# Token mixing: gated products in groups of four tiles instead of two, with the rest of a batch's work one place later

## The reference, cut to what matters

```python
q = x @ Wq + bq
k = x @ Wk + bk
v = x @ Wv + bv
scores = jnp.einsum('btd,bsd->bts', q, k)
retained = jnp.einsum('bts,bsd->btd', d_gamma_batched * scores, v)
y = retained @ Wo + bo
out = jnp.where(y >= 0, y, prelu_a * y)
```

## Time and profile before

| | us |
|---|---|
| median of 3 runs | 3925.51 (3924.63 to 3928.59) |
| the profiled execution's own time | 3921.38 |
| its span, first to last instruction | 3919.6 |
| mixing: starts of the first gating and of the last step (L589) | 40.74 and 396.84 |
| from one batch's `yT` to the next, undisturbed (226.80 to 247.25) | 20.45 |
| mean granted TensorE clock | 0.986 |

### The profile page before, as it was taken

One profiled execution on the slowest core, in us unless ns is written; L12 is line 12 of the kernel. 1 busy time (PEld: TensorE's weight loads), 2 busy tenths in 40 slices (PEclk: granted clock), 3 DMA queues, 4 the chain that ended last, 5 costly groups with the idle time before them and its releaser, 6 DMA issues. The chain is left out here.

```text
span 3919.6 us, 159989 instructions
## 1 busy us (share of the span) xinstructions
PE 3750.3 (96%) x61932; PEld 2749.2 (70%) x61932; DVE 3139.5 (80%) x21227; ACT 2391.9 (61%) x11882; POOL 85.4 (2%) x129
## 2 busy tenths in 40 slices
PE   7899999999999999999999899999999999999998
PEld 3333888888888888888888666666666666666664
DVE  6999899999999999999998677766777667776675
ACT  3232898888889889888887344444444443444443
POOL 6100000000000000000000000000000000000000
PEclk8999999999999999999999999999999999999999
DMA  3111000000000000000000000000000000000000
GB/s 91 22 25 23 3 3 3 3 3 3 3 3 3 3 3 3 3 3 3 3 3 4 4 8 8 8 6 6 8 8 8 6 7 7 8 8 6 6 8 7
DMA packets 49571, 34.01 MB, mean 9 GB/s; under 512 B 37661, under 2 KB 46877, under 8 KB 48806
## 3 DMA queue, kind: packets, MB, share of 16 engines
q1 hardware_dynamic: 48806, 23.77, 2.3%
HBM read 15.37 MB, written 8.39 MB: 6 GB/s over the span
## 5 line engine op out<-in xcount | busy, mean ns | idle before, releaser
L740 PE MATMUL bank<-xs,ident 128*128 128x128 f16 x15583 | 1415.1, 223 | 0.0
L740 PEld LDWEIGHTS bank<-xs,ident 128*128 128x128 f16 x15583 | 1010.2, 102 | 252.2 <-issue 229.8
L760 ACT ACTIVATE ifg_cell_dec<-bank 128x48 f32<-128x48 f32 x1024 | 215.2, 210 | 641.3 <-PE bank L752 641.3
L752 PE MATMUL bank<-enc_lo,u_hi 128*128 128x16 f16 x8192 | 530.1, 173 | 0.3 <-DVE enc_lo L812 0.3
L749 PE MATMUL bank<-enc_hi,u_lo 128*128 128x16 f16 x8192 | 527.8, 173 | 0.0
L775 DVE SCALAR_TENSOR_TENSOR terms_dec<-ifg_cell_dec 128x32 f32<-128x32 f32 x1024 | 197.1, 193 | 398.3 <-ACT ifg_cell_dec L760 387.2
L749 PE MATMUL bank<-enc_hi,u_hi 128*128 128x16 f16 x8192 | 501.6, 170 | 0.0
L749 PEld LDWEIGHTS bank<-enc_hi,u_lo 128*128 128x128 f16 x8192 | 338.4, 96 | 205.6 <-DVE enc_hi L806 171.2
L767 ACT ACTIVATE bank<-twice_cell_dec 128x16 f32<-128x16 f32 x1024 | 191.7, 187 | 402.4 <-DVE twice_cell_dec L781 402.4
L752 PEld LDWEIGHTS bank<-enc_lo,u_hi 128*128 128x128 f16 x8192 | 339.3, 96 | 67.9 <-DVE enc_lo L812 0.4
L749 PE MATMUL bank<-ring_hi,u_lo 128*128 128x16 f16 x4096 | 260.7, 172 | 102.3 <-DVE ring_hi L806 96.0
(11 more groups left out here) (268 smaller groups left out, 7900.8 us busy)
## 6 DMA issues: line engine op xcount, KB each, us to landing
g_rows<-tok_d_gamma_batched_dram SPq DMA_DIRECT2D x8, 512.0 KB, 6.5
x_rows<-in_x_dram SPq DMA_DIRECT2D x16, 256.0 KB, 3.0
kept_h<-tok_ln_h SPq DMA_DIRECT2D x32, 128.0 KB, 2.1
res<-kept_h SPq DMA_DIRECT2D x32, 128.0 KB
out_dram<-sums SPq DMA_DIRECT2D x32, 128.0 KB
raw_wd<-in_L_attn_Wd_dram SPq DMA_DIRECT2D x2, 256.0 KB
raw_experts<-in_L_ffn_W_dram SPq DMA_DIRECT2D x2, 256.0 KB
raw_u<-in_L_attn_Uf_dram SPq DMA_DIRECT2D x1, 256.0 KB
```

The lines of the kernel that those rows point to most:

```text
L740: nc.tensor.matmul(spare, m.ident16[:], m.xs[:, 0, :, :].rearrange("p b t -> p (b t)"), start=False, stop=True, skip_group_check=True)
L752: last = nc.tensor.matmul(z[k], m.u_hi[c.d][:, g, :], h_lo, start=False, stop=True, skip_group_check=True)
L760: nc.scalar.activation(c.ifg_cell[:, 0:3, :], ifg, ACT.Tanh, scale=1.0 / Z_SCALE).then_inc(c.s_t_ifg, 1)
```

## The change

Products are issued in groups of four tiles: at places 3, 7, 11 and 15 of a batch, the group of tiles t - 7 to t - 4. Before, a pair of tiles t - 3 and t - 2 was issued at each odd place. At place 3 the group is thus tiles 12 to 15 of the batch before. `G_RING` goes from 6 to 8. Every piece of `post` on PE, ACT and DVE is moved from place t to t + 1, because the last products of a batch now come at place 3. `Z_RING` stays 3, `prep` stays where it was, and no arithmetic is added or taken out.

```diff
     Z_RING = 3
-    G_RING = 6
+    G_RING = 8
+    GROUP = 4
...
-                def product_pair(n):
-                    pe.wait_ge(s_g, n + 2)
-                    product(*divmod(n, NT))
-                    product(*divmod(n + 1, NT))
+                def product_group(n):
+                    pe.wait_ge(s_g, n + GROUP)
+                    for k in range(n, n + GROUP):
+                        product(*divmod(k, NT))
 
                 def products(b, t):
 
-                    n = NT * b + t - 3
-                    if t % 2 and n >= 0:
-                        product_pair(n)
+                    n = NT * b + t + 1 - 2 * GROUP
+                    if n >= 0 and n % GROUP == 0:
+                        product_group(n)
 
                 def last_products():
-                    product_pair(NT * B - 2)
+                    product_group(NT * B - GROUP)
...
                 def post(b, t):
                     k = b % 2
-                    if t == 3:
+                    if t == 4:
                         pe.wait_ge(s_yT, b + 1)
...
-                    if t == 2:
+                    if t == 3:
                         act.wait_ge(s_av, NT * (b + 1))
                         S.activation(yT[:], m.bank[3 + k][:], ACT.Identity, bias=m.bo_col[:, 0:1]).then_inc(s_yT, 1)
...
-                    if t == 4:
+                    if t == 5:
                         latest[:] = [Own(dve, s_own, LINKS * b)]
                         own = latest[0]
```

More of the change, by code:

```diff
@@ L521, in post @@
                         last.then_inc(s_y, 1)
-                    if t == 13:
+                    if t == 14:
                         pe.wait_ge(s_n, b + 1)
@@ L577, in post @@
                     k = b % 2
-                    if t == 2:
+                    if t == 3:
                         act.wait_ge(s_av, NT * (b + 1))
                         S.activation(yT[:], m.bank[3 + k][:], ACT.Identity, bias=m.bo_col[:, 0:1]).then_inc(s_yT, 1)
-                    if t == 9:
+                    if t == 10:
                         act.wait_ge(s_var, b + 1)
                         S.activation(ln.dev[:], ln.var[:], ACT.Sqrt).then_inc(s_sd, 1)
-                    if t == 11:
+                    if t == 12:
                         act.wait_ge(s_nm, b + 1)
                         S.activation(ln.split[:, :, 0:D], ln.square[:], ACT.Identity).then_inc(s_nh, 1)
-                    if t == 14:
+                    if t == 15:
                         act.wait_ge(s_nT, b + 1)
@@ L646, in post @@
                     own = latest[0] if latest else None
-                    if t == 5:
+                    if t == 6:
                         own.wait()
@@ L651, in post @@
                             ).then_inc(s_h, 1)
-                    if t == 6:
+                    if t == 7:
                         dve.wait_ge(s_h, b + 1)
@@ L656, in post @@
                         own.made(TS(ln.mean[:], ln.total[:], 1.0 / D, None, ALU.mult))
-                    if t == 7:
+                    if t == 8:
                         own.wait()
                         own.made(TT(ln.centred[:], ln.h[:], over_tokens(ln.mean[:]), ALU.subtract))
-                    if t == 8:
+                    if t == 9:
                         own.wait()
                         own.made(TT(ln.square[:], ln.centred[:], ln.centred[:], ALU.mult))
-                    if t == 9:
+                    if t == 10:
                         own.wait()
@@ L667, in post @@
                         TS(ln.var[:], ln.squares[:], 1.0 / D, EPS, ALU.mult, ALU.add).then_inc(s_var, 1)
-                    if t == 10:
+                    if t == 11:
                         dve.wait_ge(s_sd, b + 1)
@@ L683, in post @@
                         assert own.n == LINKS, own.n
-                    if t == 12:
+                    if t == 13:
                         dve.wait_ge(s_nh, b + 1)
```

## The result

The changed kernel takes 3950.8 us (median of 4 runs, 3949.2 to 3954.9) against 3925.1 beside it; the ratio is 1.0064, with a 95% interval of 1.0049 to 1.0079. It is slower by 25.7 us where 20.2 were forecast. The time lies inside the range, 4.8 us above the forecast of 3946, and where the dearer of the two loops had been put (3950), the rival with a chance of 0.20.

The account below looks back on a forecast made before the run. PE was taken to bound the mixing, DVE close behind. Eleven steps 15.0, step without next batch 0.9, last step 0.9, first three batches 3.4: 20.2 us on 3921.38, plus 4.1 for the median, gives 3946 us; range 3935 to 3955.

Parts of the forecast that it names:

- the dearer of the two loops: Rival: a group's first product ends late, at 1.08 us; 0.3 us more a batch, about 3950 us; chance 0.20.
- What bounds: Mixing before the change: PE sets the pace at 20.45 us a batch, DVE's own floor being 19.28.
- DVE's leg: DVE from the start of `neg` to the end of gating tile 14: 13.69 us, one gating less than 14.29.
- What is saved: PE's products: a group of four costs 1.965 us instead of 2.22, saving 1.0 us a batch.
- PE keeps the pace: Rival: PE still ahead of DVE at tile 14, batch falls to 19.45 us, run 3909.5 us; chance 0.05.
- PE's leg: From the end of gating tile 14, through PE's scores, two groups and turning `yT`, to `neg`'s start: 8.12 us.
- Does DVE keep up during PE's leg: Check after tile 14: first product ready 0.65 us after its pair starts, tile 1 gated 0.2 us before needed.
- DVE's idle places: DVE idle twice a batch: 1.1 us before gating tile 4, for a product, and 1.4 us before `neg`.
- the forecast loop: Waits between DVE and PE close a round trip of 21.81 us a batch, 1.36 longer than before; chance 0.68.
- The step without a next batch: Mixing step to 369.95, with no transposes of x for a next batch: 21.36 against 20.45, 0.9 us longer.
- The last step: End of mixing: four pairs behind the layernorm's transposes where it had three, 0.9 us longer.
- The first three batches: Mixing beside POOL: 3.4 us added, 2 x 1.36 plus half for the first; bounds 0 and 4.3 on top.

Follow-up runs that it names:

- the places re-laid: Changed kernel with groups two places earlier, x turned at place 3, vo at 7, neg at 5, layernorm's end one later: ratio 0.9984 to before; with pairs 1.0000.

## Why the prediction was right, and where its sizes were off

**What bounds.** Right: the pair of runs with one DVE operation less shows PE as the pace before and DVE's leg on the path after.

**What is saved.** Right: 1.965 us for a group, 1.0 us a batch on PE. The rival that let this saving through (PE keeps the pace, 3909.5) needed a trip of 19.45; it was 22.35.

**DVE's leg.** Right: 13.69.

**PE's leg, 8.12 forecast, 8.66 measured.** The step that failed is the one in "Does DVE keep up during PE's leg": there I took the early end of a group's first product, 0.65 us after the group's start, because two of the four records of a pair end there, and put the late end at 1.08 among the rivals. The group of place 15 starts at 253.38 and the gating that needs its first product starts at 254.56, 1.18 later; the one of place 3 starts at 257.92 and the gating of tile 4 at 259.10, again 1.18. So the first product of a pair comes no earlier than about 1.1 us, with the second. The trace of the kernel before could have settled this. Each product is two records, and the four records of a pair run two by two (the pair of the earlier trace rows at 246.10, in stretches cut between its records):

```profile
246.10 0.65 PE L489 MATMUL bank<-gated,vo 128*64 128x512 f32 x2
246.58 0.60 PE L489 MATMUL bank<-gated,vo 128*64 128x512 f32 x2
```

Only the later two carry the step of the semaphore `products_made`, and its events in that trace come at 247.18 and 247.23, which is 1.09 and 1.13 us after the pair's start. The two records that end at 0.65 are the first halves of both products, not the first product. Hence tile 0 starts 1.85 after the gating of tile 14 instead of 1.25 (the rows gave 1.36 even without a wait: 0.03 and 0.73 us for `k`, 0.60 for tile 15; the slip of 0.1 changed nothing), tile 1 ends at 256.45, and the scores of tile 4 start at 256.51, 0.39 after PE had been free for them (255.25 + 0.44 + 0.43 = 256.12). The rival had 0.3 for this. Ten buffers take the cause away, and 0.40 us comes back. The rest of the 0.54 is small: the scores of tile 1 start 0.15 behind the gating instead of 0.06, and `neg` 0.70 behind the transposes instead of 0.64. Why, I can't say.

**DVE's idle places.** Forecast 1.1 before tile 4 and 1.4 before `neg`; measured 1.46 and 0.98, and 0.40 before tile 0. Their sum is 2.84 against 2.5; with the later first product, waiting moved from before `neg` to before tile 4. DVE idle before tile 0 was what I had named as a sign against the forecast loop and for the dearer one.

**The sum.** Eleven steps: 15.0 forecast, 20.9 measured, by the leg above. The step without a next batch: 0.9 forecast, 1.15. The last step: 0.9, 0.85. The first three batches: 3.4 forecast, 1.3 measured. It lies between "swallowed" (0) and the undisturbed price, but that is luck: three of the ten experiments end this part 5.6 to 6.8 us sooner than the kernel before, which the bounds put on this term had no room for. In all 20.2 against 24.2 in the mixing stage. That the dearer loop's 3950 fits so well is in part luck too: it added 0.3 us a batch to the trip of 21.81 where 0.54 came, and the first three batches gave back 2.1 of the 3.4. The 25.7 of the timed medians and the 24.2 agree within what runs scatter (3949.2 to 3954.9 and 3919.4 to 3928.6).

**The three parts of the loss,** which the prediction did not separate, are a matter of the experiments: later place of `post` 0.45, lateness of the last products 0.50, four in a row 0.95 (0.40 of it the ring), in sum 1.90 us a batch. All were measured as steps taken in this order; in another order the shares differ: with the places re-laid, four in a row gains 0.27 us a batch (20.52 to 20.25).

## What to carry to other kernels

Where two engines are within a few per cent of each other, as here with 20.45 and 19.28 us a batch, work taken from the busier one is worth at most the distance between them (1.17 us here, room for the whole 1.0), and only if the order doesn't make a loop out of them. Before batching small operations for one engine, walk the chain that closes from one round to the next (here `neg`, gating, scores, last products, `yT`, `neg`) with start-to-start times of the trace, and see what stood between its links that the new order takes out. The first of two overlapping products frees its buffer about when the second does; look for the record that carries the semaphore's step, not for the first that ends. Here the batched group paid only once the work around it had been laid anew, which took a batch from 22.35 to 20.25 us against 20.45 before. And judge such a gain by the undisturbed steps: of the 8.5 us by which that kernel's mixing stage ended sooner, 6.8 came from the part beside POOL.

## What the runs showed of the hardware

Two f32 products in the two halves of the array's columns run side by side: their records start together, two by two 0.43 to 0.48 us apart, eight in 1.94 us, 0.855 us a pair. The semaphore steps come 1.09 and 1.13 us after the pair's start, and DVE starts on the first's buffer at 1.18. Getting into the half-width f32 products and out again, from f16 matmuls of full width, costs 0.25 us, once for a pair or for four. The element type alone does not cost it on the way in: the full-width f32 transposes start a normal 0.215 us after the f16 matmul ahead of them. On the way out no run parts type and width. The Trainium skill (TensorEngine Tiling (Array Packing), Tiling Modes, Key Properties) has such a drain at every change of tiling mode; the trace agrees in that it is paid once per group, whatever the group's length.

While POOL works on long three-partition operations, some DVE operations last until POOL's end and others don't. Kernel before, in order of time, beside the earlier trace rows:

```profile
91.08 1.51 POOL L321 CAST bias_part<-bias_left 3x1608 bf16<-3x1608 f32 x1
91.39 0.68 DVE L654 TENSOR_REDUCE tok_ln_total<-tok_ln_h 128x8 f32<-128x512 f32 x1
92.10 0.52 DVE L656 TENSOR_SCALAR tok_ln_mean<-tok_ln_total 128x8 f32<-128x8 f32 x1
92.54 0.68 DVE L632 TENSOR_TENSOR gated<-bank,gammaT 128x512 f32<-128x512 f32 x1
92.70 4.33 POOL L327 TENSOR_SCALAR bias_left<-bias_part,ident 3x1608 f32<-3x1608 bf16 x1
...
93.14 3.44 DVE L659 TENSOR_TENSOR tok_ln_centred<-tok_ln_h,tok_ln_mean 128x512 f32<-128x512 f32 x1
```

The reduction at 91.39 keeps its 0.68 us beside POOL; the small scaling at 92.10 lasts until POOL's cast ends at 92.59, and the subtraction at 93.14 runs 3.44 us, to 96.58, while POOL's scaling ends at 97.03. Which operands or operations are held back, and for how long when it is not until POOL's end, was not tried. Where the operations fall beside POOL's differs from kernel to kernel, and the third `yT` with it, by up to 8.4 us. That this is also why the change cost only 1.3 us there is likely, but no run shows it.
